# Attention scores contracted over all 128 rows, with constant rows below the operands, written by GpSimd at the start

## The reference

```python
qkv = x @ Wqkv + bqkv
q, k, v = jnp.split(qkv, 3, axis=-1)      # 16 heads of 8
q, k = rope(q), rope(k)
scores = jnp.einsum('bhqd,bhkd->bhqk', q, k) * 8 ** (-0.5)
scores = jnp.where(causal[None, None], scores, -jnp.inf)
weights = jax.nn.softmax(scores, axis=-1)
out = jnp.einsum('bhqk,bhkd->bhqd', weights, v)
```

## Time and profile before

| | |
|---|---|
| median of three runs | 819.37 us (805.48, 819.37, 820.41) |
| the profiled execution, its time | 810.94 us |
| its span, first to last instruction | 809.1 us |
| PE / DVE / ACT / POOL busy | 688.0 / 512.5 / 450.7 / 286.5 us |
| granted TensorE clock, mean | 0.878 of full |

### The profile page before, as it was taken

One profiled execution on the slowest core, in us unless ns is written; L12 is line 12 of the kernel. 1 busy time (PEld: TensorE's weight loads), 2 busy tenths in 40 slices (PEclk: granted clock), 3 DMA queues, 4 the chain that ended last, 5 costly groups with the idle time before them and its releaser, 6 DMA issues.

```text
span 809.1 us, 14402 instructions
## 1 busy us (share of the span) xinstructions
PE 688.0 (85%) x5166; PEld 328.1 (41%) x5166; DVE 512.5 (63%) x844; ACT 450.7 (56%) x896; POOL 286.5 (35%) x488
## 2 busy tenths in 40 slices
PE   3337868999979999899989999999999997999944
PEld 1125612355555336443332364334434333256613
DVE  7872398876544572577646547698899897653301
ACT  1214303655636676866656765676767774645841
POOL 3548512233100111267421114672122122015883
PEclk9558955999998999698788997899999997799965
DMA  5200563020370123003341124055132212000000
GB/s 160 68 10 1 155 169 116 28 60 27 103 188 7 35 51 78 10 1 92 122 112 43 47 61 152 2 139 147 46 86 60 56 32 61 1 1 2 1 26 27
DMA packets 33476, 52.24 MB, mean 65 GB/s; under 512 B 5888, under 2 KB 24064, under 8 KB 30848
## 3 DMA queue, kind: packets, MB, share of 16 engines
q1 hardware_dynamic: 32112, 50.87, 23.3%
q10 hardware_dynamic: 1296, 0.46, 0.2%
HBM read 37.42 MB, written 13.63 MB: 63 GB/s over the span
## 4 chain that ended last, share of the span: by engine, by line
PE 60%; DVE 16%; POOL 10%; issue 6%; ACT 5%; DMA 2%; POOLq 0%; SPq 0%; ACTq 0%; DVEq 0%
PE ps L1184 55%; DVE maxes L1170 6%; ACT probs L922 3%; DVE rope L1034 2%; POOL gate L462 2%; PE ps L1390 1%; DMA F<-in_w 1%; PE ps L1277 1%; POOL gate L799 1%; POOL gate L810 1%; ACT F L882 1%; POOL gate L811 1%; PE ps L1238 1%; DVE kop L1039 1%; PE ps L1293 1%
## 5 line engine op out<-in xcount | busy, mean ns | idle before, releaser
L1170 DVE TENSOR_REDUCE maxes<-ps 128x2 f32<-128x1024 f32 (+2 forms) x288 | 339.9, 1221 | 116.2 <-PE ps L1184 114.1
L922 ACT ACTIVATE probs<-ps 128x512 f32<-128x512 f32 x576 | 306.0, 603 | 119.4 <-PE ps L1184 118.6
L1184 PE MATMUL ps<-qop,kop 74*128 74x512 bf16 (+3 forms) x768 | 193.0, 351 | 13.8 <-ACT probs L922 7.0
L775 POOL TENSOR_SCALAR_AFFINE_SELECT probs<-probs 128x512 f32<-128x512 f32 (+1 forms) x160 | 83.5, 544 | 264.3 <-ACT probs L922 264.0
L1184 PE MATMUL ps<-probs,vgrp 128*32 128x512 f32 (+3 forms) x1536 | 160.2, 528 | 12.8 <-POOL probs L775 11.3
L1184 PE MATMUL ps<-kmx,qmx 32*128 32x128 bf16 (+2 forms) x1280 | 109.7, 282 | 27.5 <-DVE maxes L1170 14.8
L1184 PEld LDWEIGHTS ps<-qop,kop 74*128 74x128 bf16 x768 | 62.9, 103 | 119.5 <-ACT probs L922 60.3
L1184 PE MATMUL ps<-F 128*128 128x128 f32 (+3 forms) x768 | 93.5, 285 | 6.1 <-DMA F<-in_w 3.3
L1184 PEld LDWEIGHTS ps<-F 128*128 128x128 f32 (+2 forms) x768 | 85.6, 185 | 24.8 <-issue 16.3
L1184 PEld LDWEIGHTS ps<-kmx,qmx 32*128 32x128 bf16 x1280 | 39.1, 94 | 135.2 <-issue 77.0
L1184 PEld LDWEIGHTS ps<-probs,vgrp 128*32 128x32 f32 x1536 | 39.2, 113 | 73.9 <-issue 53.1
(11 more groups left out here) (154 smaller groups left out, 685.9 us busy)
## 6 DMA issues: line engine op xcount, KB each, us to landing
qop<-q_thirds SPq DMA_DIRECT2D x48, 192.0 KB
kop<-k_thirds SPq DMA_DIRECT2D x48, 192.0 KB
qmx<-q_thirds SPq DMA_DIRECT2D x16, 256.0 KB
kmx<-k_thirds SPq DMA_DIRECT2D x16, 256.0 KB
F<-in_w SPq DMA_DIRECT2D x16, 256.0 KB, 5.0
q_thirds<-third SPq DMA_DIRECT2D x8, 384.0 KB, 3.0
k_thirds<-third SPq DMA_DIRECT2D x8, 384.0 KB, 2.8
q_thirds<-third SPq DMA_DIRECT2D x8, 256.0 KB, 2.2
```

What stands on the lines that cost most here:

```text
L775: last = pool.affine_select(where, where, [[0, number], [1, P]], ALU.is_ge, 0.0, base=0, channel_multiplier=-1)
L922: act.activation(probs[:, u % RING, :], bank(at), ACT.Exp, scale=SCALE).then_inc(s_cells_read, 1)
L1170: dve.tensor_reduce(dst, src, AX.X, ALU.max).then_inc(s_units_read[pair // 2], 1)
L1184: return pe.matmul(out_, lhsT, rhs, start=first, stop=last)
```

## The change

The score products read all 128 rows of both operands. Rows 64 to 127 of `kop` are filled with ones and those of `qop` with zeros before anything else is written there; the loads then overwrite rows 64 to 73 (rows 64 to 71 by `ldexp`; 72 and 73 of `qop` by `shift`), and rows 74 to 127 add one times zero. The fills are memsets on POOL, over f32 words that hold two bf16 each (8192 bf16 a row, 4096 words), after its first three memsets, each with a wait of its own; `s_ones` is counted there. DVE's two memsets of ones are removed.

```diff
+
+ONES = float(np.array([0x3F803F80], np.uint32).view(np.float32)[0])
@@ gpsimd, before its walk over ORDER
             pool.wait_ge(s_pad, 3)
+
+            pool.memset(kop[64:P].rearrange("p r h t -> p (r h t)").bitcast(F32), ONES).then_inc(s_ones, 1)
+            pool.wait_ge(s_ones, 1)
+            pool.memset(qop[64:P].rearrange("p r h t -> p (r h t)").bitcast(F32), 0.0).then_inc(s_ones, 1)
+            pool.wait_ge(s_ones, 2)
@@ vector, embstat
                 elif kind == "embstat":
-                    for r in range(2):
-                        dve.memset(kop[64:KM, r], 1.0).then_inc(s_ones, 1)
                     dve.wait_ge(s_emb_in, 16)
@@ tensor, exp
-                        last = mm(bank(at)[:, c:c + w], kop[0:KM, r, h, P * j:P * j + P], qop[0:KM, r, h, q:q + w])
+                        last = mm(bank(at)[:, c:c + w], kop[:, r, h, P * j:P * j + P], qop[:, r, h, q:q + w])
```

## The result

The changed kernel takes 783.08 us (median of four runs, 782.38 to 783.79), the kernel before 813.63 us in the same comparison (median of four, 805.48 to 820.41). The ratio is 0.9686, with a 95% interval of 0.9636 to 0.9736. The forecast was 789 us, the range 774 to 804. Ratios leave out single runs that lay more than 1.5% above the fastest of their kernel, so that a ratio can differ a little from that of the medians.

The account below looks back on a forecast made before the run. PE was taken to bound the kernel, with DVE setting the pace at the start. From 810.9 us, less 19.1 (clock) and 8.6 (DVE memsets), plus 6.0 (POOL's hold-up), came 789.2 us; range 774 to 804.

Parts of the forecast that it names:

- the clock follows how much of the array the products fill: Attention: half clock comes behind products leaving part of the array empty; 128-row scores give back 19.1 us.
- The rival with an unchanged clock: Attention: clock follows busy time or nonzero rows, so only the front gains; 808.3 or 802.3 us, chance 0.14.
- How the low stretches begin: Attention, seven half-clock stretches, 75.1 us: some begin behind PE busy with narrow products, others behind idle PE or without scores.
- Cost of the wider products: Score products over 128 rows: same 768 products, columns and weight loads, so their own cost is taken as 0.
- The rival that loads lose their overlap: Weight loads beside 128-row scores no longer overlap, each costing 0.103 us; up to 868 us, chance 0.03.
- How much half clock goes: Attention: of 75.1 us in seven low stretches, 51.2 us go, as 20.4 + 20.5 + 10.3.
- the three that were to vanish: Low stretches at 253.0, 488.5 and 509.0 in attention should not begin at all; together 20.4 us.
- the two that I kept longer: Low stretches 420.2 and 679.6, beginning with a long PE wait and few scores: 3.5 and 6.8 us go.
- Its price: Attention: each microsecond at half clock gives back 0.37 us at full clock, from counts of exponentials, 37/59.
- VectorE's two memsets: Start: removing DVE's two memsets from 38.71 to 47.32 brings all that follows 8.6 us earlier.
- GpSimd's hold-up: Start: POOL's two memsets hold up short DVE tensor_scalars, 6.0 us late, with nothing making it up.
- the rival in which POOL doesn't hold DVE up: Start: a memset reads nothing, so DVE isn't delayed; clock as in the forecast, 783.2 us, chance 0.25.

Follow-up runs that it names:

- rows alone: Against the kernel before: score products over 128 rows, both fills on VectorE where its two memsets were, of the same length; 788.9 us, ratio 0.9725.
- front alone: Against the changed kernel: score products back to rows 0 to 73, fills still on GpSimd; 808.49 us, ratio 0.9966 to the kernel before.
- 96 rows: Against the kernel with 128-row products and both fills on VectorE: score products over rows 0 to 95; 797.79 us, ratio 0.985 to the kernel before.

## Why the prediction was right

- **That the clock follows how much of the array the products fill** was the step on which all rested, read from low stretches with a busy PE. It is shown: rows alone 0.9725, front alone 0.9966, 96 rows between (0.985). The rival with an unchanged clock (802 to 808 us) is out, in both of its forms: by busy time alone, since 96 and 128 rows differ from 74 at equal work, and by data, since no difference between zeros and random numbers can be told.
- **How the low stretches begin** I had read too simply. The prediction has three of them begin behind a PE that was busy, and all go on with PE 95% to 100% busy. In 679.6 to 696.7 PE was busy for 13.88 of 17.10 us, 81%. And of the 3.40 us ahead of 253.0, 488.5 and 509.0 it was busy for 2.57, 2.42 and 2.63 us, 71% to 77%; ahead of the other four it was less, as in the last line:

```profile
249.60:253.00 3.40, 2.57 (x30) 1.39 (x32) 3.29 (x3) 3.39 (x6) 1.59 (x4) 1.00 0.02 5
485.10:488.50 3.40, 2.42 (x29) 1.01 (x30) 3.40 (x4) 2.88 (x4) 0.00 (x0) 1.00 0.19 36
328.10:331.50 3.40, 1.18 (x9) 0.38 (x7) 2.64 (x3) 3.40 (x10) 0.45 (x2) 1.00 0.00 0
```

  So every one of the seven begins behind a PE that was idle in part, and so do the six that are left in the changed kernel's attention after 271 us (0.46 to 1.95 of 3.40 us). That idle time has a part in the fall fits all of them, but no run tests it by itself. What the runs show is that the rows count as well: at unchanged work, 55 us less at half clock.
- **Cost of the wider products: 0.** Right: 397 ns for 512 columns, and a weight load of 101 ns against 103 ns. The rival that loads lose their overlap is out; in attention PE's busy time fell, and its idle time hardly moved (642.1 - 601.3 = 40.8 us before, 619.9 - 578.2 = 41.7 after).
- **How much half clock goes.** Forecast 51.2 us. Of the seven stretches 3.4 + 10.2 + 10.3 + 6.9 + 10.2 + 6.8 + 10.3 = 58.1 us went: the three that were to vanish did, 331.5 and 379.2 shrank to 3.4 us as forecast, and the two that I kept longer shrank to 3.4 and 6.8 us instead of 6.8 and 10.3. One short stretch at 271.8 us is new. The sum is near for a reason, the match stretch by stretch is luck: with the front alone, and 74 rows, 253.0 and 488.5 vanished too, and others came for them.
- **Its price.** 0.37 us for each, from counts of exponentials. By the stages, 22.2 us for 93.2 - 38.1 = 55.1 us is 0.40. The counts gave it slightly low, if one pair of traces can tell. More low time gone (55.1 against 51.2 us) and this price make 22.2 us where 19.1 us were forecast.
- **VectorE's two memsets: 8.6 us, and 6.0 us back for GpSimd's hold-up.** Right in kind and nearly in size: line 1020 ends at 8.62 + 3.12 = 11.74 us, where its like ended at 6.10 + 0.17 = 6.27, 5.5 us late. The net was to be 2.6 us, and the slot moments moved from 47.32 to 43.28, by 4.0 us. Beside the 0.5 us of the hold-up, 0.9 us came from places that I didn't look at: at the point where the two memsets had stood, VectorE is 4.6 us late and no longer 5.5. The prediction had it that nothing makes the delay up, and part of it was made up: further on, short VectorE instructions meet GpSimd's at other moments than before. One of them is the tensor_scalar of line 1009 at 16.53 us in the kernel before, whose timeline reads

```profile
16.19 1.26 POOL L759 TENSOR_TENSOR F<-F,gam 128x512 f32<-128x512 f32 x1
16.53 0.94 DVE L1009 TENSOR_SCALAR root<-mv 128x4 f32<-128x4 f32 x1
```

  and which in the changed kernel, where GpSimd is idle at that moment, takes 0.17 us in the same chunk (the last line; those of the two chunks ahead stand above it):

```profile
16.95 0.20 DVE L1016 TENSOR_SCALAR root<-mv 128x4 f32<-128x4 f32 x1
...
19.50 0.17 DVE L1016 TENSOR_SCALAR root<-mv 128x4 f32<-128x4 f32 x1
...
21.92 0.17 DVE L1016 TENSOR_SCALAR root<-mv 128x4 f32<-128x4 f32 x1
```

  The Trainium skill's rule for the shared pair ("SBUF — State Buffer", "Who interferes with whom") agrees with the trace also in its finer part: an instruction with two SBUF inputs contends only with a GpSimd instruction that reads, and the tensor_tensor beside the memset took 0.16 us. Beside a GpSimd tensor_tensor, which reads (20.76 us in the kernel before, 1.26 us long), one of VectorE's at 20.92 us took 1.13 us.
- **The tail**, left out of the sum, gave 0.9 us.

The sum was 21.7 us, the measured change 27.6 us: 3.1 us of the difference lie in attention, 2.0 in the front (4.6 to the first score product against 2.6) and 0.9 in the tail, all in terms that were there or were left at nothing. One coincidence could mislead: 783.2 us was the number of the rival in which POOL doesn't hold DVE up, and 783.34 was measured. The timeline shows the hold-up all the same (2.70 and 3.12 us); the forecast's missing 6 us came from attention, the front and the tail as just listed.

## What to carry to other kernels

Where a stretch is at half clock while PE is busy throughout, look at how much of the array its products fill; rows that are there anyway can be named in the instruction, with zeros on one side (or on both), and the product itself took no longer here. The rows have to be filled once. Put such fills where no short VectorE instruction on the chain can meet them: a long GpSimd memset holds a VectorE tensor_scalar of four elements a partition until it ends (2.70 and 3.12 us beside memsets of 3.51 us). A transfer issued early held nothing up that could be told here: VectorE's first tensor_scalar took 0.17 us as in the kernel before, and the slot moments came at 39.03 us.

## What the runs showed of the hardware

- At 1.2 GHz PE was busy for 10.19 of 10.20 us with 74-row scores among its work. The same work named over 128 rows spends 38 us of attention at 1.2 GHz instead of 93 (mean clock 0.97 against 0.93). I had expected this; that all-zero rows count as well as random ones (ratios 0.9527 and 0.9572) I had not been sure of.
- A GpSimd memset, which reads nothing, held a VectorE tensor_scalar for 2.70 and 3.12 us, but not a reciprocal (0.18 us) nor a tensor_tensor (0.16 us).
- Cutting a fill of 4096 words into 16 costs GpSimd about a quarter more (4.2 and 4.5 us against 3.51) and takes VectorE's tensor_scalar beside it from 2.70 to 0.26 us, the wait included.
